# Expert stage of a perceiver kernel: outputs two items behind, three activation buffers, banks freed by the first multiplication

## The reference

```python
logits = xf @ gate_weight.T ; scores = sigmoid(logits)
# choose 4 of 8 groups, then 6 of 32 experts for each token
tw = tw / (tw.sum(-1) + 1e-20) * 2.5 ; combine[token, expert] = tw
def expert_step(acc, inp):
    gu, dn, c = inp
    g = xf @ gu[:I].T
    u = xf @ gu[I:].T
    return acc + c[:, None] * (silu(g) * u @ dn.T)
sh = silu(xf @ shared_gate_w.T) * (xf @ shared_up_w.T)
x = x + routed + sh @ shared_down_w.T
```

## Time and profile before

| | us |
|---|---|
| median of 3 runs | 1929.55 |
| lowest and highest | 1923.28 and 1940.96 |
| the profiled execution | 1934.74 |
| its span | 1933.0 |
| PE, DVE, ACT, POOL busy | 1753.6, 1398.0, 1242.7, 576.6 |

### The profile page before, as it was taken

The page is one execution under the profiler, slowest core; times in us unless marked ns, Lnnn a source line. Parts: engine busy times, 40 slices in busy tenths (PEclk is TensorE's granted clock), DMA queues, the critical chain, the costliest instruction groups (busy, mean ns, idle before and its releaser), DMA issues. The chain is left out here.

```text
span 1933.0 us, 68149 instructions
## 1 busy us (share of the span) xinstructions
PE 1753.6 (91%) x29700; PEld 1106.4 (57%) x29720; DVE 1398.0 (72%) x2412; ACT 1242.7 (64%) x2173; POOL 576.6 (30%) x463
## 2 busy tenths in 40 slices
PE   7899999999989587899779999999999999847898
PEld 5577777777765264434436665666665665535443
DVE  2677777777753675578478988988988997356565
ACT  3377777777743381222248888888888888447243
POOL 4322232232130441456312222222222220033365
PEclk8899999999999688899779999999999999868899
DMA  4355555555400300456465655655555652030011
GB/s 156 95 142 138 149 145 144 149 141 144 116 4 0 66 4 17 120 153 174 92 109 104 104 97 105 103 97 105 102 99 105 103 98 28 1 68 4 28 42 41
DMA packets 66556, 178.40 MB, mean 92 GB/s; under 512 B 20276, under 2 KB 24500, under 8 KB 65844
## 3 DMA queue, kind: packets, MB, share of 16 engines
q1 hardware_dynamic: 64436, 170.85, 40.0%
q10 hardware_dynamic: 1824, 3.20, 0.8%
HBM read 84.39 MB, written 1.31 MB: 44 GB/s over the span
## 5 line engine op out<-in xcount | busy, mean ns | idle before, releaser
L648 ACT ACTIVATE Pb<-ps 128x512 f32<-128x512 f32 (+1 forms) x832 | 451.9, 597 | 50.4 <-PE ps L595 31.8
L615 PE MATMUL ps<-Pb,V 128*17 128x64 f32 (+1 forms) x13312 | 380.6, 248 | 0.7 <-ACT Pb L648 0.7
L724 DVE TENSOR_REDUCE MX<-ps 128x2 f32<-128x804 f32 (+1 forms) x385 | 364.0, 984 | 18.7 <-PE ps L561 17.5
L615 PEld LDWEIGHTS ps<-Pb,V 128*17 128x17 f32 (+1 forms) x13312 | 250.6, 97 | 87.2 <-issue 43.5
L726 DVE TENSOR_REDUCE MX<-ps 128x1 f32<-128x402 f32 (+1 forms) x512 | 265.9, 569 | 30.8 <-PE ps L565 24.8
L768 POOL TENSOR_TENSOR ABO<-CT 128x1601 bf16<-128x1601 f32 x44 | 125.9, 2863 | 538.7 <-DMA CT<-ctxT 538.7
L651 ACT ACTIVATE Pb<-ps 128x1024 f32<-128x1024 f32 (+1 forms) x224 | 204.6, 959 | 40.9 <-PE ps L599 38.3
L561 PE MATMUL ps<-KST,QW 50*128 50x402 bf16 (+1 forms) x1024 | 177.9, 343 | 13.1 <-DVE MX L724 5.6
L595 PE MATMUL ps<-QW,KST 50*128 50x128 bf16 (+1 forms) x3328 | 165.4, 219 | 4.3 <-ACT Pb L648 2.4
L671 ACT ACTIVATE V<-ps 128x512 f32<-128x512 f32 (+1 forms) x256 | 129.3, 521 | 48.3 <-PE ps L547 39.8
L565 PE MATMUL ps<-KST,QW 96*128 96x402 bf16 (+1 forms) x512 | 148.0, 338 | 6.4 <-POOL QW L758 0.4
(11 more groups left out here) (261 smaller groups left out, 3228.4 us busy)
## 6 DMA issues: line engine op xcount, KB each, us to landing
CT<-ctxT SPq DMA_DIRECT2D x44, 800.5 KB, 4.7
KST<-HL SPq DMA_DIRECT2D x320, 100.1 KB, 3.0
KST<-C SPq DMA_DIRECT2D x320, 100.1 KB, 3.0
Pb<-routed SPq DMA_DIRECT2D x64, 256.0 KB, 3.9
ABO<-ctxT SPq DMA_DIRECT2D x10, 800.5 KB, 4.9
T<-ctxT SPq DMA_DIRECT2D x10, 800.5 KB, 4.4
KST<-HL SPq DMA_DIRECT2D x128, 50.0 KB, 2.7
KST<-C SPq DMA_DIRECT2D x128, 50.0 KB, 2.7
```

The lines of the kernel that those rows point to most:

```text
L615: mm = nc.tensor.matmul(ps[32 * quad:32 * quad + m, SUM, oc:oc + nh * S], V[0:n, b % 2, tile, v0:v0 + m], Pb[0:n, buffer(b, x), ti * att.W ...
L648: nc.scalar.activation(Pb[0:n, buffer(b, x), i * 512:(i + 1) * 512], score_bank(b, x, i)[0:n, :], ACT.Exp, scale=att.scale).then_inc(exps, 1)
L724: nc.vector.reduce_max(MX[:, b % 2, 2 * j:2 * j + 2], work(job)[:, :, 0:n], AX.X).then_inc(freed["dve"], 1)
```

## The change

PE's outputs run two items behind gate and up in place of one: `up(i, cc)`, then `down(i-2, cc)`. `HID` and `HLO` get a third buffer, and lie in `ABO`. `up` waits for the first multiplication of the same chunk of the item before (`mid`; for item 0, which has only one, `hid`) in place of the second. The two sweeps become one sequence of 34 items on PE, DVE and SP: PE does not drain between them, DVE adds the first sweep's output behind item 1 of the second sweep, and SP's loop runs over the 32 routed items without a break. Neither the buffers of `RW` (two), nor the slots of `CT` (four), nor the conditions of `sp_experts` and `sp_weights` are changed, nor the order of the two in SP's loop.

```diff
-            HID = [Pb[:, 1, :], spare[:, 0:4 * CH].bitcast(F32)]
-            HLO = [spare[:, (2 + u) * 2 * CH:(3 + u) * 2 * CH] for u in range(2)]
+            HID = [Pb[:, 1, :], ABO[:, 0:2 * CH], ABO[:, 2 * CH:4 * CH]]
+            HLO = [ABO[:, (4 + u) * CH:(5 + u) * CH].bitcast(BF16) for u in range(3)]
...
-                return (sweep * NI + item) % 2
+                return (sweep * NI + item) % 3
+
+            def multiplied(sweep, item, cc):
+                if item:
+                    return s["mid"], sweep * 2 * (NI - 1) + 2 * (item - 1) + cc + 1
+                return s["hid"], unit(sweep, item, cc) + 1
...
-                    eng.wait_ge(s["hid"], unit(sweep, item, cc) - 1)
+                    eng.wait_ge(*multiplied(sweep, item - 1, cc) if item else multiplied(sweep - 1, NI - 1, cc))
...
-                    if unit(sweep, item, cc) >= 4:
-                        eng.wait_ge(s["down"], unit(sweep, item, cc) - 3)
+                    if unit(sweep, item, cc) >= 6:
+                        eng.wait_ge(s["down"], unit(sweep, item, cc) - 5)
...
+            items = [divmod(i, NI) for i in range(2 * NI)]
+            if role == "pe":
+                for i, (sweep, item) in enumerate(items):
+                    for cc in range(2):
+                        up(sweep, item, cc)
+                        if i >= 2:
+                            down(*items[i - 2], cc)
...
+            if role == "dve":
+                for i, (sweep, item) in enumerate(items):
+                    dve_item(sweep, item)
+                    if i == NI + 1:
+                        dve_add(0)
+                dve_add(1)
+            if role == "sp":
+                routed = [(sweep, item) for sweep, item in items if item]
+                for sweep, item in routed[:SLOTS]:
+                    sp_experts(sweep, item)
+                eng.wait_ge(s["weights"], NC)
+                eng.dma_start(ROUTED, BYE).then_inc(stored, 16)
+                eng.wait_ge(stored, 16)
+                for i, (sweep, item) in enumerate(routed):
+                    sp_weights(sweep, item)
+                    if SLOTS <= i + 2 < len(routed):
+                        sp_experts(*routed[i + 2])
```

More of the change, by code:

```diff
@@ L1430, in moe_stage @@
             WL = ABO[:, 3 * N:4 * N].bitcast(BF16)[:, 0:SLOTS * 3 * D].rearrange("p (s n) -> p s n", s=SLOTS)
-            spare = QW[:, :, :].rearrange("p a n -> p (a n)")
-            HID = [Pb[:, 1, :], spare[:, 0:4 * CH].bitcast(F32)]
-            HLO = [spare[:, (2 + u) * 2 * CH:(3 + u) * 2 * CH] for u in range(2)]
+            HID = [Pb[:, 1, :], ABO[:, 0:2 * CH], ABO[:, 2 * CH:4 * CH]]
+            HLO = [ABO[:, (4 + u) * CH:(5 + u) * CH].bitcast(BF16) for u in range(3)]
             def upper(x):
@@ L1595, in dve_item, with dve_add @@
                     ins.then_inc(s["hid"], 1)
+            def dve_add(sweep):
+                for cc in range(2):
+                    eng.wait_ge(s["down"], unit(sweep, NI - 1, cc) + 1)
+                    x = ck(X, 2 * sweep + cc)
+                    nc.vector.tensor_tensor(x, x, ps[:, cc, :], ALU.add).then_inc(s["out"], 1)
             def sp_experts(sweep, item):
@@ L1618, in moe_stage @@
                 eng.wait_ge(ready[0], ready[1])
[L1619 to L1623, removed]
+            items = [divmod(i, NI) for i in range(2 * NI)]
+            if role == "pe":
+                for i, (sweep, item) in enumerate(items):
+                    for cc in range(2):
+                        up(sweep, item, cc)
+                        if i >= 2:
+                            down(*items[i - 2], cc)
+                    if i == 0:
                         eng.wait_ge(s["parts"], 1)
-                        for i, bank in enumerate(turned_banks):
+                        for k, bank in enumerate(turned_banks):
                             for t in range(4):
-                                tr = nc.tensor.matmul(ps[0:E, bank, t * 128:(t + 1) * 128], TW[:, 4 * i + t, :], w("ident"),
+                                tr = nc.tensor.matmul(ps[0:E, bank, t * 128:(t + 1) * 128], TW[:, 4 * k + t, :], w("ident"),
                                                       start=True, stop=True)
                             tr.then_inc(s["turned"], 1)
[L1630 to L1633, removed]
+                for sweep, item in items[-2:]:
                     for cc in range(2):
[L1635 to L1639, removed]
+                        down(sweep, item, cc)
+            if role == "act":
+                for sweep, item in items:
+                    act_item(sweep, item)
+            if role == "pool":
+                for sweep in range(2):
                     pool_weights(sweep, 1)
```

## The result

The changed kernel took 1945.32 us (median of 20 runs, 1934.19 to 1955.92), the kernel before 1931.49 us (median of 20, 1923.28 to 1942.43). The ratio is 1.0069, interval 1.0054 to 1.0085: 13 us slower. I had forecast 4.7 us slower, in a range of 1920 to 1940. The direction was right; the size was too small by more than half, and the time lies outside the range. (The forecast of 1934 was counted from the median of three runs, 1929.55; the median of 20 lies 1.9 us higher.)

A forecast was written before the change was run, and what follows sets the result against it. The prediction took PE as nearly full, stopped by waits for the second multiplication. Stops of 13.4 us from SP's delay less 8.7 us removed gave +4.7 us on 1929.55, so 1934, range 1920 to 1940.

The forecast's parts named there:

- The loop that binds: Routing weights, DVE's multiplications, POOL's rest and weight split, `up`: 13.37 us for three items against 11.76 without a stop.
- The long stops: PE waiting for POOL's weight split: one stop of 1.6 us every third item, eight in the stage.
- the pace P = 3.92 us: Time of one item in the expert stage if PE never waited, against 4.12 us in the kernel before.
- What the change removes: Waits for the second multiplication 5.6 us, the stop between the sweeps 2.3, the head 0.8: 8.7 us in all.
- Their cover is the 2 us by which DVE is ahead: First sweep's additions in DVE's list cost nothing thanks to DVE's lead; without it at most 2 x 0.69 us.
- T(i): Time when PE has done `up(i,1)` and `down(i-2,1)` and could start `up(i+1,0)`.
- How often: four loops.: Items 3 to 16, 13 intervals, hold four three-item loops, each with a stop of 1.6 us; the second sweep four more.
- The head: Start of the stage: `up(2,0)` need not wait for the first routing weights; 0.8 us gained.
- Rival (c): PE's clock falls at the new stops in the stage: slower by over 1%, 1994 if in half the items; chance 0.03.
- (a): SP's delay does not bind, so the full gain of 8.7 us comes: 1920.9; chance 0.22 with halfway cases.
- (b): Gain and stops in the stage cancel within 2 us: about 1929; chance 0.08.
- (d): Banks are not freed earlier, something else gates `up`, so only the stops are added: 1939.9; chance 0.07.

The follow-up runs named there:

- the swap: The changed kernel with SP issuing the routing transfers of item i+1 ahead of the expert transfer of item i+2; ratio to the kernel before 0.999.
- eight slots: The changed kernel with eight slots for expert weights in place of four, loads four items ahead in place of two; ratio to the kernel before 1.0.
- the kernel before with SP's wait alone: The kernel before with SP waiting for one more item of outputs before each expert transfer, no other part of the change; ratio 1.0137.
- the kernel before with the early release alone: The kernel before with `up` waiting for the routed item before's first multiplication in place of its second, nothing else; ratio 0.9992.

## Why the prediction was wrong in size, step by step

**Right.** SP's wait moves back by one item and the routing transfers stand behind it (the swap, eight slots, and the kernel before with SP's wait alone). The routing weights come 5.01 us behind the expert transfer's issue, where 4.87 was worked out. The loop that binds is the one by way of POOL's split: 13.54 us for three items against 13.37. The two stops between the sweeps for POOL, 2.06 us, are gone. The second multiplication no longer stops `up`.

**Right only in part.** The second multiplication waits 1.6 us for each routed item on average, 26 waits and 41.1 us in all, and not 2.1: where PE itself has been stopped, the multiplication is asked for later. The long stops do not come at every third item either, but at items 6, 9, 11 and 14 of the first sweep.

**The step that failed is the gain, with the pace P = 3.92 us under it and the additions put at nothing.** "What the change removes" was 8.7 us. With SP's wait out of the way (eight slots) the stage is 4.2 us shorter than before. Against that kernel the changed one is 14.1 us longer, where the stops were worked out as 13.4. So 4.5 us of the 5.2 us by which the sum was short (9.9 measured, 4.7 forecast) are the gain, and 0.7 are the stops. The missing 4.5 us, one by one:

- 2.6 us: the pace. P was read from PE's matmuls alone, with VectorE and GpSimd taken to keep up. Without POOL's weight split the stage is 2.6 us shorter. The kernel before with the early release alone says the same: 5.6 us were put down for the waits that it removes, 4.8 expected of it, 0.5 came. The rows of before had the hold-up in front of me, a second multiplication of 0.69, 0.91 and 1.13 us beside POOL's work; I used these numbers as durations and did not ask whether DVE and POOL, so slowed, could follow PE at 3.92.
- 1.0 us (1.2 and 0.9 by the two profiles): the additions. "Their cover is the 2 us by which DVE is ahead": there was none. The stop is as long in the kernels whose routing weights are not late, so it does not come from SP's delay. DVE's list has the additions behind the second multiplications of the second sweep's item 1. The last of these started at 870.29, only 1.4 us behind the silu of the same unit (868.93), with no wait for a DMA in between, so the additions could not be done by the time PE asked for them.
- 0.7 us: the sum on paper. A stage built from its own parts (17.1 to item 3, then 57.4, 17.5 and 61.5, with all stops as forecast) comes to 153.5 us, where 148.1 + 4.7 is 152.8.

That is 4.3 of the 4.5 us; the rest is less than two profiles of one kernel differ.

**Where the time shows in the changed kernel itself**, from T(i) as SP's expert transfers mark it. Here the short stops cannot be told from the loop, so the same error lies elsewhere:

- "How often: four loops." I charged four stops of 1.6 us to 13 intervals, though 4.46 - 3.92 = 0.54 us for each of 13 is 7.0 us, not 6.4. From item 3 to 16 the profile has 860.01 - 801.18 = 58.8 us where 13 x 3.92 + 6.4 = 57.4 was forecast: +1.5 us, 0.6 of it this count and 0.7 the loop's 0.17 us. In the loop shown above the landing is 0.14 us longer, the second multiplication with the way to POOL 0.12 and the way from the split to PE 0.08; DVE's two starts before are 0.19 shorter.
- From item 16 to 20 there are 18.9 us where 17.5 was forecast (with the f32 matmuls of item 0): +1.3 us, 1.0 of it PE's wait for the addition. The rest is the stop ahead of item 1 of the second sweep, 0.9 us in place of 0.6, 0.4 of it a wait for POOL's split.
- The second sweep from item 20 to the end: 942.47 - 878.87 = 63.6 us against 61.5: +2.1 us, 1.7 of it in the 13 items and 0.4 in the tail.
- The head came 0.4 us earlier than forecast.

Together 4.5 us, and the 0.7 us of the sum on paper make 5.2.

**The clock.** Rival (c) did not occur: from 796 to 942 us of the changed kernel the granted clock is 1.00, so the new stops did not lower it. But what (c) has against itself, that the trace had not shown such a fall in this stage, is wrong. In the head, behind PE's wait for the first `up` of a routed item, it was at its lower level: 0.50 from 787 to 792 us in the kernel before (PE had waited 3.7 us) and 0.51 from 787 to 793 us in the changed one. In the repeat of the kernel before it was 1.00 from 787 us on. And the kernel before with SP's wait alone shows the fall in the midst of the stage, behind a stop of 3.2 us. Both stops are about three times as long as the longest that SP's delay made in the changed kernel, 1.1 us.

**The other rivals.** (a), SP's delay does not bind, and (b), the halves cancel, did not happen. (d), only the stops, gave 1939.9, nearest of my cases; that is luck, since the banks were freed early as planned. The figure of the Trainium skill for a transfer (DMA: Bandwidth & Descriptors, section "Anatomy of one DMA"), an estimate of 2.6 us for 256 KB, would have given eight stops of 0.2 us; the rows' 4.0 us were right (3.4 to 5.0, median 4.0, in the changed kernel). That "this trace disagrees with the page" holds for the transfers that spread a row over 64 partitions only: the one other transfer of 256 KB in the stage, `routed<-C`, landed in 2.6 us before and after.

**The range** ended at (d). The stage alone, 9.9 us above the median of 20, would have passed it. The high end of the landing, which I had worked out, and the noise of a median went into it only once, and nothing in it allowed for a cover that fails.

## What to carry to other kernels

When outputs are moved back on the engine that computes, look for every queue that waits on their semaphore: what stands behind that wait moves back too, and here it was a transfer that had nothing to do with it. Issue first what has less time to spare, or give the waiting transfer more buffers; either took back the whole loss. And before counting on an engine's bare pace, follow the engines that feed it through an item at the durations that the trace shows when they run beside each other: a hold-up that costs nothing while the first engine waits anyway shows as soon as that wait is taken away.

## What the runs showed of the hardware

- A 128x512 f32 multiplication with both operands in SBUF took 0.69 us alone and up to 1.31 us when it began just behind a POOL operation; with one operand in PSUM it took 0.68 to 0.69 us beside the same POOL work.
- How long an expert transfer of 192 KB takes to land depends on what goes out around it: 2.3 us at the median (3.3 at most) with no routing transfers beside it, 2.5 and 2.6 in the changed kernel and the one before (3.6 and 4.5 at most), 2.8 in the swapped one (4.9 at most), and 4.0 with eight slots, where it is issued right behind two routing transfers. A schedule that gives it 0.3 us to spare shows the late ones.
- A transfer of 256 KB that spreads one row over 64 partitions landed in 4.0 us at the median, the plain one of 256 KB in 2.6.
- PE's granted clock stayed at 1.00 through stops of 1.1 us among 13.5 us of work. It fell to 0.52 behind one stop of 3.2 us (905.5 to 909 us, SP's wait alone in the kernel before).
- Two profiles of one kernel agreed within 0.4 us in the length of this stage (one of four of the changed kernel was 1.5 us off), while whole executions of one kernel spread over 20 us. The stage's length could mostly tell 1 us apart; twelve timed runs, with intervals of 0.2%, could hardly tell 4.
